# Selective scan: two of four summed terms move from TensorE to VectorE, and two sets of DMAs move in SyncE's queue

## The chip, the cores and the metric

One core of one Trainium2 chip runs the whole program. The metric is device microseconds of one execution. The profile comes from one further execution. Engines are called by the profile's names: PE is TensorE, DVE VectorE, ACT ScalarE, POOL GpSimd, SP SyncE, which here only issues DMAs.

## The reference

The program is four layers on x (4 batches of 512 tokens, 512 channels, fp32): a selective scan, a gated FFN with 4-bit weights, a cross attention, a ternary FFN, a mixing attention, a ternary FFN with norms, a second selective scan and a routed attention. The change touches only the two selective scans. For each batch they compute

```python
x = einsum('ed,bld->bel', in_proj_w, hidden)         # 512 channels x 512 steps
u = silu(depthwise_conv(x, 4 taps) + conv_b)
x_dbl = einsum('ke,bel->bkl', x_proj_w, u)           # rows: dt_low 16, B 16, C 16
delta = softplus(einsum('er,brl->bel', dt_proj_w, dt_low) + dt_proj_b)
state = state * exp(delta * A) + (delta * u) * B     # 512 steps, 16 states per channel
y = sum over states of state * C + D * u             # then times silu(z), added to x
```

softplus(v) is computed as max(v, 0) + log(1 + e), with e = exp(-|v|). Since 1 + e is rounded before the logarithm, the kernel adds the rounding error back: e + (1 - (1 + e)). So delta is a sum of four arrays: e, one-less = 1 - (1 + e), the logarithm, and the positive part.

## The kernel before, in words

`stage_mamba` runs twice, as "m0" (first scan stage, `then` set) and as "m3" (second, `given` set). Each goes through 4 batches b of NU = 32 units k. A unit is one state n of one half of the channels (2 blocks of 128 channels, 512 steps each), so n = 32 b + k counts units. In a unit ACT makes two decays `dA` (L757) into 3 PSUM banks, POOL makes the inputs `dB` = du * B (L777, 128x1024), DVE runs two scans (L827, L836) and one product with C (L844), POOL makes the other product (L766, 128x512), and PE adds both products to y in PSUM with an identity matmul (L570, L578). In units 5, 12, 21 and 28 DVE makes both products itself (L850). POOL writes `dB` up to four units ahead, but its queue holds dB(n), then product(n - 2), which waits for the scans of unit n - 2.

While batch b is scanned, the same engines prepare batch b + 1 at fixed units, given by tuples: projection, convolution, `xdbl`, step, and then delta. ACT makes |v| and the positive part, e (at units 21 and 22, into `xin`), one-more and one-less (22 to 24, into `du`), and the logarithm of both halves (24, into `delta`). PE then sums the four arrays for each of the 4 channel blocks ("sum", units `SUM`, two PSUM banks shared by everything that PE prepares), DVE multiplies a sum by u (`times_u`, L807, units `TIMES_U`) and ACT copies it out (`copy_sum`, L694, units `COPY_SUM`). A bank is free for the next item but one only when both have read it. The first stage prepares its batch 0 ahead of the loop, where nothing is being scanned, and prepares a fifth batch during its last one, which the second stage starts from; that one has 3 more to prepare. So 7 of the 8 batches have a preparation inside them. In m0's batch 2, PE and ACT also transpose and copy the next stage's weights (`REWEIGH`, L512 to L516, L621 to L625), among the same two banks.

SP loads B and C of a unit (`rows_of`, L427) into one of 5 buffers when the products of the unit five before are done. The rows come from DRAM: SP stores `xdbl` of a batch at the start of that batch (L445), waits until the store has landed, and goes on to the loads. In m0's batch 1 it first issues 8 loads of the next stage's weights.

Of the kernel before, what the change touches and what calls it, by code (L numbers as in the profile page):

```python
# [12 lines left out]
ALU = mybir.AluOpType  # L13
# [4 lines left out]
B, L, D = 4, 512, 512  # L18
# [277 lines left out]
def stage_mamba(chip, name, bc_dram, weights, then=None, given=None):  # L296
# [7 lines left out]
    EH = EB // 2  # L304
    FIRST, NB = 1 if given else 0, B + 1 if then else B
    NU = 2 * N
    with ExitStack() as st:
# [46 lines left out]
        s_dbl, s_dblc, s_bcd = sem("xdbl"), sem("xdbl_copied"), sem("bc_stored")  # L354
        s_relu = sem("relu")
        s_dt, s_ab, s_e, s_ln = sem("dt"), sem("dt_abs"), sem("dt_exp"), sem("dt_ln")
        s_one, s_back, s_sum, s_del, s_du = sem("one_more"), sem("one_less"), sem("summed"), sem("delta"), sem("du")
        s_bc = [sem(f"bc_loaded{i}") for i in range(NS)]
        s_dA, s_dB, s_sc = sem("dA"), sem("dB"), sem("scanned")
        s_hd, s_hp, s_ho = sem("product_dve"), sem("product_pool"), sem("product_own")  # L360
# [5 lines left out]
        GATED = (1, 3)  # L366
        PROJECT, TURN, CONV, XDBL, STEP = (0, 1, 2, 3), (5, 6, 11, 12), (7, 8, 9, 10), 13, (16, 17, 18, 19)
        SILU, EXP, ONE, BACK, LOG = (10, 13), (21, 22), (22, 23), (23, 24), 24
        SUM, TIMES_U, COPY_SUM = (24, 25, 27, 28), (26, 27, 29, 30), (28, 29, 31, 31)
        LAG = 3  # L370
        ROOT, INVERSE = 5, 7

        REWEIGH = {(0, 1): (0, 1), (0, 2): (2, 3)} if given else {(2, k): (i,) for i, k in enumerate((20, 21, 22, 25))} if then else {}
# [37 lines left out]
        @block.sync  # L411
        def _(sp):
            def park_or_load(i, h):
                part = parked[i][:, h * EH:(h + 1) * EH, :]
                here = (u, delta, du)[i][0][:, h * EH:(h + 1) * EH, :]
                if given:
                    sp.dma_start(here, part).then_inc(s_given[h] if i else s_gu, 16)
                else:
                    sp.dma_start(part, here).then_inc(s_park, 16)

            def rows_of(b, k):
                n, src = b * NU + k, bc_parked if b < FIRST else bc_dram[b]
                if n >= NS:
                    sp.wait_ge(s_hd, n - NS + 1)
                    sp.wait_ge(s_hp, n - NS + 1 - owned(n - NS + 1))
                    sp.wait_ge(s_ho, owned(n - NS + 1))
                sp.dma_start(BC[n % NS][:], src.rearrange("(w n) t -> n w t", w=2)[k % N:k % N + 1].broadcast_to(  # L427
                    [P, 2, L])).then_inc(s_bc[n % NS], 16)

            if given:  # L430
                weights.load_small(sp)
                for i in (2, 1):
                    park_or_load(i, 0)
                for k in range(2):
                    rows_of(0, k)
                park_or_load(0, 0)
                weights.load_rows(sp)
                for k in range(2, NS):
                    rows_of(0, k)
                for i in (2, 1, 0):  # L440
                    park_or_load(i, 1)
            for b in range(NB):
                if b >= FIRST:
                    sp.wait_ge(s_dblc, b + 1)
                    sp.dma_start(bc_parked if b == B else bc_dram[b], xdbl[R:W, :]).then_inc(s_bcd, 16)  # L445
                    sp.wait_ge(s_bcd, 16 * (b + 1 - FIRST))
                if b == B:
                    sp.wait_ge(s_du, NB * EB)
                    sp.wait_ge(s_del, NB * EB)
                    for i in range(3):  # L450
                        for h in range(2):
                            park_or_load(i, h)
                    sp.wait_ge(s_park, 96)
                    break
                if then and b == 1:
                    sp.wait_ge(s_wt, 1)
                    nxt.load_small(sp)
                    nxt.load_rows(sp)
                for k in range(NS if b < FIRST else 0, NU):
                    rows_of(b, k)  # L460

        def first_weights(pe):
            pe.wait_ge(weights.s_rows, weights.ROWS)
# [13 lines left out]
        def _(pe):  # L477
# [26 lines left out]
            def work(kind, b, i):  # L504
# [13 lines left out]
                elif kind == "project":  # L518
                    if i == 0 and b >= (FIRST if given else B):
                        pe.wait_ge(s_wgc, KC + 2)  # L520
                    for k in range(KC):
                        m = pe.matmul(out, in_T[:, k, i * P:(i + 1) * P],
                                      ctxT[:, k, b % B * L:(b % B + 1) * L], start=(k == 0), stop=(k == KC - 1))
                    m.then_inc(s_x, 1)
                elif kind == "conv":
                    pe.wait_ge(s_xin, b * EB + i + 1)
                    if given:
                        pe.wait_ge(s_pad, 2)
                        pe.wait_ge(s_diag, EB * TAPS)
                    elif b == B:  # L530
                        pe.wait_ge(s_diag, 2 * EB * TAPS)
                    for k in range(TAPS):
                        m = pe.matmul(out, taps[:, i, k, :], xin[:, i, k:k + L], start=(k == 0), stop=(k == TAPS - 1))
                    m.then_inc(s_conv, 1)
                elif kind == "xdbl":
                    pe.wait_ge(s_u, (b + 1) * EB)
                    for e in range(EB):
                        m = pe.matmul(out[0:W], x_T[:, e, :], u[b % 2][:, e, :], start=(e == 0), stop=(e == EB - 1))
                    m.then_inc(s_dbl, 1)
                elif kind == "step":  # L540
                    pe.wait_ge(s_dblc, b + 1)
                    pe.matmul(out, dt_T[:, i * P:(i + 1) * P], xdbl[0:R, :], start=True, stop=True).then_inc(s_dt, 1)
                elif kind == "sum":
                    pe.wait_ge(s_relu, b * EB + i + 1)
                    pe.wait_ge(s_back, 2 * b + i // EH + 1)
                    pe.wait_ge(s_ln, b + 1)
                    pe.matmul(out, ident[:], xin[:, i, TAPS - 1:], start=True, stop=False)
                    pe.matmul(out, ident[:], du[b % 2][:, i, :], start=False, stop=False)
                    pe.matmul(out, ident[:], delta[b % 2][:, i, :], start=False, stop=False)
                    pe.matmul(out, ident[:], positive[:, i, :], start=False, stop=True).then_inc(s_sum, 1)  # L550
                else:
                    for j in range(EH):
                        pe.wait_ge(s_yz[j], 2 * (b + 1))
                    for e in range(EB):
                        m = pe.transpose(out[:, e * P:(e + 1) * P], gate(b)[:, e, i * P:(i + 1) * P], ident[:])
                    m.then_inc(s_yt, 1)
# [228 lines left out]
        def _(dve):  # L785
# [11 lines left out]
                if not given:  # L797
                    diagonals(e, weights.small)
            if given:
                dve.sem_inc(s_du, EB)  # L800
            dve.wait_ge(s_pad, 2)
            norm.moments(dve)

            def times_u(b, e):
                dve.wait_ge(s_sum, b * EB + e + 1)
# [45 lines left out]

            if not given:
                norm.inverse(dve)
                for e in range(EB):
                    times_u(0, e)
            for b in range(B):
                for k in range(NU):
# [4 lines left out]
                    if b and k - 2 in TURN:  # L862
                        add_y(b - 1, TURN.index(k - 2))
                    if b + 1 < NB:
                        if k in TIMES_U:
                            times_u(b + 1, TIMES_U.index(k))
                    n = b * NU + k
# [2229 lines left out]
```

## Time and profile before

| | us |
|---|---|
| median of 3 runs | 4154.32 (4152.64 to 4157.45) |
| the profiled execution, its own time | 4150.07 |
| its span | 4148.3 |
| busy in the span: PE, DVE, ACT, POOL | 3649.8, 2860.9, 1818.7, 1435.3 |
| m0, starts of DVE's first and last unit | 96.08, 567.24 |
| m3, the same | 3160.05, 3607.62 |

A row of the timeline gives start, duration, engine, line, operation, output and inputs, and in brackets how long the engine had been idle before it and what ended the wait. Durations of neighbours on one engine overlap by about 0.1 us, so the pace of an engine is read from starts.

### The profile page before, as it was taken

What the parts mean: (1) busy time and instruction counts of PE and PEld (TensorE: products, weight loads), DVE (VectorE), ACT (ScalarE), POOL (GpSimd) and SP (SyncE); (2) the same over time, 40 slices, a digit from 0 to 9 for tenths busy, and PEclk for the clock granted to TensorE, in tenths of its full rate; (3) what the DMA queues carried; (4) which work ended last, traced back from release to release, by engine and by line L of the source; (5) the groups of instructions that cost most, each with busy time, mean ns of one, the idle gap of its engine ahead of it and who ended that gap; (6) DMA issues with size and microseconds to landing.
All of it is one profiled execution on the core that took longest, in us unless ns stands there. A gap on an engine that the chain in (4) does not pass through costs nothing. (4 is left out here: it accounts for less than half of the span.)

```text
span 4148.3 us, 47410 instructions
## 1 busy us (share of the span) xinstructions
PE 3649.8 (88%) x15419; PEld 1758.1 (42%) x15419; DVE 2860.9 (69%) x4137; ACT 1818.7 (44%) x3051; POOL 1435.3 (35%) x1030
## 2 busy tenths in 40 slices
PE   6999856999999999898999879785886999689898
PEld 2333323555555555542333344343333333244454
DVE  2888888578777884457888256627667899934663
ACT  4666542222222221243777443336665666321244
POOL 1999854122211220054000100003445999700122
PEclk8999987999999999997999989896998999899999
DMA  3555441122233212365775110001004555502420
GB/s 100 141 155 147 129 127 57 50 93 74 68 103 100 81 31 74 116 144 102 79 79 56 55 61 0 3 0 64 10 0 130 149 151 148 141 18 71 80 56 22
DMA packets 249833, 338.37 MB, mean 82 GB/s; under 512 B 45602, under 2 KB 147522, under 8 KB 248036
## 3 DMA queue, kind: packets, MB, share of 16 engines
q1 hardware_dynamic: 249620, 335.70, 32.5%
q8 instruction: 112, 1.84, 0.2%
q14 instruction: 101, 0.83, 0.1%
HBM read 284.38 MB, written 53.35 MB: 81 GB/s over the span
## 5 line engine op out<-in xcount | busy, mean ns | idle before, releaser
L757 ACT ACTIVATE m_dA<-m_delta,m_a_neg 128x512 f32<-128x512 f32 x512 | 347.2, 689 | 328.1 <-DVE m_H_bank L827 255.3
L1926 DVE TENSOR_REDUCE a_core_minus_max<-a_core_a 128x1 f32<-128x512 f32 x512 | 317.1, 684 | 57.2 <-PE a_core_a L1752 57.2
L570 PE MATMUL m_y<-m_H,ident 128*128 128x512 f32 x512 | 279.9, 634 | 80.9 <-DVE m_H L844 80.3
L777 POOL TENSOR_TENSOR m_dB<-m_du,m_BC 128x1024 f32<-128x1024 f32 x128 | 301.6, 2357 | 123.3 <-DVE m_du L807 84.7
L766 POOL TENSOR_TENSOR m_H<-m_H,m_BC 128x512 f32<-128x512 f32 x224 | 285.0, 1272 | 63.5 <-DVE m_H L836 60.6
L1878 ACT ACTIVATE X<-a_core_s 128x512 f32<-128x512 f32 x512 | 264.6, 603 | 92.7 <-PE a_core_s L1752 92.6
L777 POOL TENSOR_TENSOR XN<-m_du,m_BC 128x1024 f32<-128x1024 f32 x128 | 301.3, 2361 | 2.7 <-DMA m_BC<-bc_ready 2.7
L1318 POOL TENSOR_TENSOR ctxT<-ctxT,f_scales 128x1024 f32<-128x1024 f32 x48 | 103.7, 2159 | 531.7 <-DVE ctxT L1143 531.7
L578 PE MATMUL m_y<-m_H,ident 128*128 128x512 f32 x512 | 271.5, 619 | 2.5 <-POOL m_H L766 2.4
L1278 ACT ACTIVATE XN<-f_g,f_power_back 128x512 f32<-128x512 f32 x128 | 88.0, 687 | 404.1 <-PE f_g L1215 404.1
L1384 DVE SCALAR_TENSOR_TENSOR XN<-f_u,f_power_back,XN 128x512 f32<-128x512 f32 x128 | 95.8, 749 | 226.9 <-PE f_u L1215 226.9
L1289 ACT CAST f_inter_high<-XN 128x512 fp32r<-128x512 f32 x128 | 79.5, 621 | 383.5 <-DVE XN L1384 383.5
L1752 PE MATMUL a_core_a<-a_core_k,a_core_q 96*128 96x512 bf16 x512 | 209.2, 411 | 23.8 <-ACT a_core_max_rows L1896 10.1
L1205 PE MATMUL f_acc<-f_wdown_high,f_inter_high 128*128 128x512 f32 x512 | 224.1, 438 | 0.0
L1207 PE MATMUL f_acc<-f_wdown_high,f_inter_low 128*128 128x512 f32 x512 | 202.7, 396 | 0.0
L1326 POOL TENSOR_TENSOR XN<-f_mag,ctxT 128x1024 f32<-128x1024 f32 x48 | 127.7, 2660 | 215.8 <-DVE f_mag L1152 109.8
L1206 PE MATMUL f_acc<-f_wdown_low,f_inter_high 128*128 128x512 f32 x512 | 202.2, 395 | 0.0
L1213 PE MATMUL f_g<-f_xn_high,f_wh 128*128 128x512 f16 x512 | 196.5, 384 | 1.4 <-ACT f_wh L1191 1.4
L1752 PE MATMUL a_core_s<-a_core_q,a_core_k 98*128 98x512 bf16 x512 | 192.0, 386 | 4.8 <-ACT X L1878 4.5
L1213 PE MATMUL f_u<-f_xn_high,f_wh 128*128 128x512 f16 x512 | 194.6, 380 | 1.4 <-ACT f_wh L1191 1.4
L1214 PE MATMUL f_g<-f_xn_low,f_wh 128*128 128x512 f16 x512 | 195.1, 381 | 0.0
L1215 PE MATMUL f_g<-f_xn_high,f_wl 128*128 128x512 f16 x512 | 195.1, 381 | 0.0
(419 smaller groups left out, 8321.9 us busy)
## 6 DMA issues: line engine op xcount, KB each, us to landing
m_BC<-bc_rows SPq DMA_DIRECT2D x224, 512.0 KB, 4.9
XN<-in_L_ffn_w_dram SPq DMA_DIRECT2D x72, 256.0 KB, 2.7
m_BC<-bc_ready SPq DMA_DIRECT2D x32, 512.0 KB, 4.9
ternary<-ctxT SPq DMA_DIRECT2D x96, 128.0 KB, 1.7
a_core_q<-a_q_parts SPq DMA_DIRECT2D x48, 256.0 KB, 12.9
a_core_k<-a_k_parts SPq DMA_DIRECT2D x48, 256.0 KB, 14.6
f_w_tern<-ternary SPq DMA_DIRECT2D x24, 512.0 KB, 6.1
f_core_q<-f_q_parts SPq DMA_DIRECT2D x24, 512.0 KB, 8.1
```

Of the source, the lines that this page charges most:

```text
L570: pe.matmul(ps_y[:, 0, :], ident[:], HD[n % NH], start=False, stop=True, skip_group_check=True).then_inc(s_ad, 1)
L578: pe.matmul(ps_y[:, 1, :], ident[:], HP[n % NH], start=False, stop=True, skip_group_check=True).then_inc(s_ap, 1)
L757: act.activation(dA[:, i % NA, :], delta[b % 2][:, e, :], ACT.Exp, scale=a_neg[:, e, k % N:k % N + 1]).then_inc(s_dA, 1)
L766: pool.tensor_tensor(HP[n % NH], HP[n % NH], BC[n % NS][:, 1, :], ALU.mult).then_inc(s_hp, 1)
L777: pool.tensor_tensor(dB[n % ND][:], du[b % 2][:, h * EH:(h + 1) * EH, :], BC[n % NS][:, 0:1, :].broadcast_to([P, EH, L]), ALU.mult).then_i ...
L1205: pe.matmul(ps_acc[:, t, :], high, DH[gb][:, q % 4, :], start=(q % 4 == 0), stop=False)
L1206: pe.matmul(ps_acc[:, t, :], high, DL[gb][:, q % 4, :], start=False, stop=False)
L1207: m = pe.matmul(ps_acc[:, t, :], low, DH[gb][:, q % 4, :], start=False, stop=(q % 4 == 3))
L1213: pe.matmul(out, w[0], xh[:, k, toks], start=(k == 0), stop=False)
L1752: pe_last = pe.matmul(out[:, cols], lhs(c, k), rhs(c, k), start=(c == 0), stop=(c == NCH - 1 and mask is None))
L1878: act.activation(prob[pair][e][:, j, q0:], ps_s[:, at % NR, q0:], ACT.Exp, scale=hs.scale).then_inc(s_exp, 1)
L1926: dve.tensor_reduce(mx[u % 2][:, qt, h:h + 1], ps_a[:, at % NR, 0:n], AX.X, ALU.max, negate=True).then_inc(s_red, 1)
```

## The change

`error` is new: for each half of the channels (128x1024) DVE adds e to one-less in place, waits for its own result, and adds the positive part in place. Both operands of both adds lie in SBUF. It runs for the next batch ahead of the scans of units 24 and 25. PE's sum has two matmuls left. `SUM`, `TIMES_U` and the first `COPY_SUM` units move one unit later. SP stores `xdbl` of batch b + 1 ahead of the load for unit 22 of batch b and waits for it only at the batch's start; the 8 loads of the next stage's weights come behind unit 8's load of batch 1.

```diff
-        SUM, TIMES_U, COPY_SUM = (24, 25, 27, 28), (26, 27, 29, 30), (28, 29, 31, 31)
-        LAG = 3
+        ERROR, SUM, TIMES_U, COPY_SUM = (24, 25), (25, 26, 27, 28), (27, 28, 29, 30), (29, 30, 31, 31)
+        LAG, STORE = 3, 22
...
-            for b in range(NB):
+            def store_rows(b):
+                sp.wait_ge(s_dblc, b + 1)
+                sp.dma_start(bc_parked if b == B else bc_dram[b], xdbl[R:W, :]).then_inc(s_bcd, 16)
+
+            if not given:
+                store_rows(0)
+            for b in range(B):
                 if b >= FIRST:
-                    sp.wait_ge(s_dblc, b + 1)
-                    sp.dma_start(bc_parked if b == B else bc_dram[b], xdbl[R:W, :]).then_inc(s_bcd, 16)
                     sp.wait_ge(s_bcd, 16 * (b + 1 - FIRST))
...
                 for k in range(NS if b < FIRST else 0, NU):
+                    if k == STORE and b + 1 < NB:
+                        store_rows(b + 1)
                     rows_of(b, k)
+                    if then and (b, k) == (1, NU // 4):
+                        sp.wait_ge(s_wt, 1)
+                        nxt.load_small(sp)
+                        nxt.load_rows(sp)
...
-                    pe.wait_ge(s_back, 2 * b + i // EH + 1)
+                    pe.wait_ge(s_err, 2 * b + i // EH + 1)
                     pe.wait_ge(s_ln, b + 1)
-                    pe.matmul(out, ident[:], xin[:, i, TAPS - 1:], start=True, stop=False)
-                    pe.matmul(out, ident[:], du[b % 2][:, i, :], start=False, stop=False)
-                    pe.matmul(out, ident[:], delta[b % 2][:, i, :], start=False, stop=False)
-                    pe.matmul(out, ident[:], positive[:, i, :], start=False, stop=True).then_inc(s_sum, 1)
+                    pe.matmul(out, ident[:], du[b % 2][:, i, :], start=True, stop=False)
+                    pe.matmul(out, ident[:], delta[b % 2][:, i, :], start=False, stop=True).then_inc(s_sum, 1)
...
+            def error(b, h):
+                rows = slice(h * EH, (h + 1) * EH)
+                t = du[b % 2][:, rows, :]
+                dve.wait_ge(s_back, 2 * b + h + 1)
+                dve.tensor_tensor(t, t, xin[:, rows, TAPS - 1:], ALU.add).then_inc(s_eh, 1)
+                dve.wait_ge(s_relu, b * EB + (h + 1) * EH)
+                dve.wait_ge(s_eh, 2 * b + h + 1)
+                dve.tensor_tensor(t, t, positive[:, rows, :], ALU.add).then_inc(s_err, 1)
...
+                for h in range(2):
+                    error(0, h)
                 for e in range(EB):
                     times_u(0, e)
...
+                        if k in ERROR:
+                            error(b + 1, ERROR.index(k))
                         if k in TIMES_U:
                             times_u(b + 1, TIMES_U.index(k))
```

On DVE, in m0's batch 0, units 23 to 27 stand so before (two scans and a product are a unit; the unit of BC3 is 23, that of BC4 is 24):

```order
L844 TENSOR_TENSOR m0_H<-m0_H_bank,m0_BC3 128x512
L827 SCALAR_TENSOR_TENSOR m0_H_bank<-m0_dA,m0_dB0 128x512
L836 SCALAR_TENSOR_TENSOR m0_H<-m0_dA,m0_dB0 128x512
L844 TENSOR_TENSOR m0_H<-m0_H_bank,m0_BC4 128x512
L827 SCALAR_TENSOR_TENSOR m0_H_bank<-m0_dA,m0_dB1 128x512
L836 SCALAR_TENSOR_TENSOR m0_H<-m0_dA,m0_dB1 128x512
L844 TENSOR_TENSOR m0_H<-m0_H_bank,m0_BC0 128x512
L807 TENSOR_TENSOR m0_du1<-m0_w,m0_u1 128x512
```

The same place on DVE with the change, where XN as an input of an add is the positive part:

```order
L860 TENSOR_TENSOR m0_H<-m0_H_bank,m0_BC3 128x512
L815 TENSOR_TENSOR m0_du1<-m0_du1,m0_xin 128x1024
L818 TENSOR_TENSOR m0_du1<-m0_du1,XN 128x1024
L843 SCALAR_TENSOR_TENSOR m0_H_bank<-m0_dA,m0_dB0 128x512
L852 SCALAR_TENSOR_TENSOR m0_H<-m0_dA,m0_dB0 128x512
L860 TENSOR_TENSOR m0_H<-m0_H_bank,m0_BC4 128x512
L815 TENSOR_TENSOR m0_du1<-m0_du1,m0_xin 128x1024
L818 TENSOR_TENSOR m0_du1<-m0_du1,XN 128x1024
L843 SCALAR_TENSOR_TENSOR m0_H_bank<-m0_dA,m0_dB1 128x512
L852 SCALAR_TENSOR_TENSOR m0_H<-m0_dA,m0_dB1 128x512
L860 TENSOR_TENSOR m0_H<-m0_H_bank,m0_BC0 128x512
```

Two adds of 128x1024 stand ahead of unit 24's scans and two ahead of unit 25's, and the first times_u no longer follows unit 25 but unit 26.

On PE, in m0's batch 2, around the last reweigh item (L516, the weights `dt_rows`), the order before is:

```order
L547 MATMUL m0_w<-m0_xin,ident 128x512
L548 MATMUL m0_w<-m0_du1,ident 128x512
L549 MATMUL m0_w<-m0_delta1,ident 128x512
L550 MATMUL m0_w<-XN,ident 128x512
L578 MATMUL m0_y<-m0_H,ident 128x512
L570 MATMUL m0_y<-m0_H,ident 128x512
L516 MATMUL m0_w<-ident,m0_dt_rows 16x128 x4
L547 MATMUL m0_w<-m0_xin,ident 128x512
L548 MATMUL m0_w<-m0_du1,ident 128x512
L549 MATMUL m0_w<-m0_delta1,ident 128x512
L550 MATMUL m0_w<-XN,ident 128x512
```

And with the change:

```order
L524 MATMUL m0_w<-ident,m0_dt_rows 16x128 x4
L555 MATMUL m0_w<-m0_du1,ident 128x512
L556 MATMUL m0_w<-m0_delta1,ident 128x512
L584 MATMUL m0_y<-m0_H,ident 128x512
L576 MATMUL m0_y<-m0_H,ident 128x512
L555 MATMUL m0_w<-m0_du1,ident 128x512
L556 MATMUL m0_w<-m0_delta1,ident 128x512
```

The first sum stood ahead of the reweigh item and now stands behind it, so the second sum's bank is no longer the one that the first sum used, but the one that the reweigh item used.

## Rows read from the trace of the kernel before

**Rows 1.** The page: the span

```profile
span 4148.3 us, 47410 instructions
```

**Rows 2.** Tile m_H_bank: what ended DVE's idle time (us, times)

```profile
  ACT m_dA L757: 71.1, 98
...
  POOL m_dB L777: 5.2, 13
```

**Rows 3.** Timeline, DVE, m0's batch 1: last product of unit 23, units 24, 25

```profile
297.48 0.67 DVE L844 TENSOR_TENSOR m_H<-m_H_bank,m_BC 128x512 f32<-128x512 f32 x1
...
300.67 1.23 DVE L827 TENSOR_TENSOR_SCAN m_H_bank<-m_dA,m_dB 128x512 f32<-128x512 f32 x1 [2.52 <-ACT m_dA L757]
...
303.79 1.23 DVE L827 TENSOR_TENSOR_SCAN m_H_bank<-m_dA,m_dB 128x512 f32<-128x512 f32 x1 [0.20 <-ACT m_dA L757]
```

**Rows 4.** Timeline, POOL, the same stretch

```profile
296.35 2.35 POOL L777 TENSOR_TENSOR m_dB<-m_du,m_BC 128x1024 f32<-128x1024 f32 x1
298.67 1.26 POOL L766 TENSOR_TENSOR m_H<-m_H,m_BC 128x512 f32<-128x512 f32 x1
299.89 2.35 POOL L777 TENSOR_TENSOR XN<-m_du,m_BC 128x1024 f32<-128x1024 f32 x1
303.09 1.27 POOL L766 TENSOR_TENSOR m_H<-m_H,m_BC 128x512 f32<-128x512 f32 x1 [0.85 <-DVE m_H L836]
```

**Rows 5.** Timeline, the 4-bit FFN: POOL beside DVE with all operands in SBUF

```profile
687.35 2.95 POOL L1326 TENSOR_TENSOR XN<-f_mag,ctxT 128x1024 f32<-128x1024 f32 x1 [4.10 <-issue]
...
687.96 2.89 DVE L1139 TENSOR_SCALAR ctxT<-f_packed 128x1024 int32<-128x1024 int32 x1
...
692.18 1.93 POOL L1318 TENSOR_TENSOR ctxT<-ctxT,f_scales 128x1024 f32<-128x1024 f32 x1 [1.89 <-DVE ctxT L1143]
...
692.19 2.47 DVE L1374 TENSOR_TENSOR f_inter_low<-XN,f_inter_high 128x512 fp32r<-128x512 f32 x1
...
696.56 1.23 DVE L1152 SCALAR_TENSOR_TENSOR f_mag<-ctxT,f_mag 128x1024 f32<-128x1024 int32 x1
```

**Rows 6.** Timeline, the last ternary FFN: two POOL products in a row, DVE's copy

```profile
2922.57 3.41 POOL L2877 TENSOR_TENSOR f_h_gained<-XN 128x512 f32<-128x512 f32 x2 [2.08 <-DVE XN L2904]
...
2924.85 1.15 DVE L2894 COPY f_gate_up_scale<-f_gate_up_scale 128x2 f32<-128x2 f32 x1
...
2925.93 1.27 POOL L2877 TENSOR_TENSOR f_h_gained<-XN 128x512 f32<-128x512 f32 x1
```

**Rows 7.** Timeline, SP, POOL and DVE at m0's border from batch 0 to 1

```profile
195.79 0.46 SPq L445 DMA_DIRECT2D bc_rows<-m_xdbl  x1
...
204.46 17.82 SPq L427 DMA_DIRECT2D m_BC<-bc_rows  x6
...
211.21 2.35 POOL L777 TENSOR_TENSOR m_dB<-m_du,m_BC 128x1024 f32<-128x1024 f32 x1 [5.36 <-issue]
...
213.59 1.23 DVE L827 TENSOR_TENSOR_SCAN m_H_bank<-m_dA,m_dB 128x512 f32<-128x512 f32 x1 [1.97 <-POOL m_dB L777]
...
220.67 1.23 DVE L827 TENSOR_TENSOR_SCAN m_H_bank<-m_dA,XN 128x512 f32<-128x512 f32 x1 [0.62 <-POOL XN L777]
```

**Rows 8.** Timeline, DVE and ACT in m0's batch 2, units 24 to 30

```profile
420.82 1.23 DVE L827 TENSOR_TENSOR_SCAN m_H_bank<-m_dA,m_dB 128x512 f32<-128x512 f32 x1 [4.39 <-ACT m_dA L757]
...
429.74 0.56 ACT L694 COPY m_delta<-m_w 128x512 f32<-128x512 f32 x1
...
436.30 0.69 DVE L807 TENSOR_TENSOR m_du<-m_w,m_u 128x512 f32<-128x512 f32 x1 [6.01 <-PE m_w L550]
...
448.31 0.69 DVE L807 TENSOR_TENSOR m_du<-m_w,m_u 128x512 f32<-128x512 f32 x1 [0.85 <-PE m_w L550]
```

**Rows 9.** Timeline, DVE and PE ahead of m0's loop: sums and times_u

```profile
76.80 2.04 PE L547 MATMUL m_w<-m_xin,ident 128*128 128x512 f32 x2 [11.77 <-ACT m_delta L689]
...
78.60 0.17 DVE L257 SCALAR_TENSOR_TENSOR m_norm_shift<-m_norm_mv,m_norm_rstd 128x16 f32<-128x16 f32 x1
...
92.31 0.69 DVE L807 TENSOR_TENSOR m_du<-m_w,m_u 128x512 f32<-128x512 f32 x1 [2.74 <-PE m_w L550]
```

More of the change, by code:

```diff
@@ L356, in stage_mamba @@
         s_dt, s_ab, s_e, s_ln = sem("dt"), sem("dt_abs"), sem("dt_exp"), sem("dt_ln")
-        s_one, s_back, s_sum, s_del, s_du = sem("one_more"), sem("one_less"), sem("summed"), sem("delta"), sem("du")
+        s_one, s_back, s_err, s_sum, s_del, s_du = (sem(n) for n in (
+            "one_more", "one_less", "error", "summed", "delta", "du"))
+        s_eh = sem("error_half")
         s_bc = [sem(f"bc_loaded{i}") for i in range(NS)]
@@ L441, in _ @@
                     park_or_load(i, 1)
-            for b in range(NB):
+            def store_rows(b):
[4 more added lines that the diff above has]
+            for b in range(B):
                 if b >= FIRST:
-                    sp.wait_ge(s_dblc, b + 1)
-                    sp.dma_start(bc_parked if b == B else bc_dram[b], xdbl[R:W, :]).then_inc(s_bcd, 16)
                     sp.wait_ge(s_bcd, 16 * (b + 1 - FIRST))
[L447 to L458, printed above, removed]
                 for k in range(NS if b < FIRST else 0, NU):
+                    if k == STORE and b + 1 < NB:
+                        store_rows(b + 1)
                     rows_of(b, k)
+                    if then and (b, k) == (1, NU // 4):
+                        sp.wait_ge(s_wt, 1)
+                        nxt.load_small(sp)
+                        nxt.load_rows(sp)
+            if then:
+                sp.wait_ge(s_du, NB * EB)
+                sp.wait_ge(s_del, NB * EB)
+                for i in range(3):
+                    for h in range(2):
+                        park_or_load(i, h)
+                sp.wait_ge(s_park, 96)
+                sp.wait_ge(s_bcd, 16 * NB)
         def first_weights(pe):
@@ L799, in _ @@
             if given:
-                dve.sem_inc(s_du, EB)
+                for sem_, count in ((s_eh, 2), (s_err, 2), (s_du, EB)):
+                    dve.sem_inc(sem_, count)
             dve.wait_ge(s_pad, 2)
             norm.moments(dve)
+            def error(b, h):
[6 more added lines that the diff above has]
+                dve.tensor_tensor(t, t, positive[:, rows, :], ALU.add).then_inc(s_err, 1)
             def times_u(b, e):
@@ L853, in _ @@
                 norm.inverse(dve)
+                for h in range(2):
+                    error(0, h)
                 for e in range(EB):
```

## The prediction

> **What bounds the kernel now.** The change touches the two scan stages alone, some 960 us of the span [rows 1], so I read these. First the tile view of the PSUM bank that DVE's scans write, because every unit passes through DVE's two scans and product: of its idle time there, ACT's decays ended 71.1 us and POOL's dB 5.2 us [rows 2]. Then the timelines of DVE and POOL side by side at units 23 to 25, where the adds go. With nothing in the way a DVE unit repeats every 3.12 us (300.67 to 303.79) [rows 3]. POOL's pair, dB and product, repeats every 3.54 us (296.35 to 299.89), but it skips the product in 4 of 32 units and waits 0.85 us for a scan here [rows 4]. So DVE sets the pace, in part through ACT: ahead of unit 24 it stands 2.52 us, because ACT makes the logarithm before unit 24's decays [rows 3]. POOL is almost without a gap. It is not the bound, but nearly so, and it is nearly always inside an instruction. That matters for what follows.
>
> **Price of an add.** DVE has no 128x1024 add with both inputs in SBUF before. The nearest row with the same shape and two SBUF inputs took 1.23 us [rows 5]. The question is what it costs beside POOL. There DVE's L1374 (128x512, two SBUF inputs) was issued 0.01 us behind a POOL product and took 2.47 us; POOL's ended at 694.11, DVE's at 694.66 [rows 5]. So DVE stood until POOL was through, then ran its 0.55 us. The other way round, POOL's product at 687.35 took 2.95 us, 0.60 more than the 2.35 of its kind in [rows 4], while DVE's L1139, issued at 687.96 right behind another DVE instruction, took 2.89 us and ended 0.55 us after POOL's [rows 5]. So a waiting POOL gets in between two DVE instructions. And a waiting DVE gets in between two of POOL: the copy of 2 elements issued at 2924.85 ended at 2926.00, with POOL's second product, and not after its third, which started at 2925.93 [rows 6]. The scans and products of the loop have one operand in PSUM, and POOL runs beside them unhindered [rows 3, 4]. The adds have none there. I take strict turns: an add waits for POOL's running instruction, runs about 1.1 us from its end, and POOL's next waits that long.
>
> The Trainium skill has two statements on this. "SBUF — State Buffer", section "Who interferes with whom", says that a DVE instruction with two SBUF inputs and a GpSimd one that reads SBUF exclude each other for a whole instruction; by it the sum is the one below. "Advanced Engine Details and Errata", section "VectorE Performance Modes", names only two-port modes as interfering, in which an fp32 add of two tensors does not run; by it the change would cost what the first rival gives. The trace agrees with the first: L1374 took 2.47 us.
>
> **Unit 24's pair**, at m0's batch 1. DVE issues the first add when the product of unit 23 is nearly through (298.07). POOL's dB ends at 298.70. The add runs to about 299.8; POOL's product, which would have started at 298.67, to 301.0; the second add, which must wait for the first, to 302.15. The scan then starts at 302.1 in place of 300.67: the 2.52 us stall for ACT hides most of it, +1.4.
>
> **Unit 25's pair** has no cover. POOL's dB, which started at 299.89, now runs from 302.15 to 304.5, its product of unit 24 (which needs that unit's second scan, through at 304.4) to 305.7. DVE's unit ends at 304.9; the first add waits to 305.7 and runs to 306.8; POOL's next dB takes the port until 309.2; the second add ends at 310.3. The scan of unit 25 starts there in place of 303.79: +6.5 in all, +5.1 from this pair. Afterwards POOL waits for unit 25's scan, so it is not late itself; it has lost 4 x 1.1 us of 113 and the gap of 0.85, while DVE lost 6.5, so DVE stays the bound. Behind DVE, ACT's three PSUM banks, PE's y adds and SP's loads of B and C all follow at the new pace.
>
> Six batches are of this kind (m0's 0, 1, 3; m3's 0, 1, 2): 6 x 6.5 = +39. Where within POOL's instruction the first add falls moves this by about 1 us a batch.
>
> **m0's batch 2.** ACT is busier, DVE's wait ahead of unit 24 is 4.39 us (scan at 420.82) and hides the first pair but for 0.9 us; the second costs 5.0. But the 6.01 us that DVE waits ahead of unit 27 for the second sum [rows 8] should go. That sum needed the bank of the first, which ACT's copy freed at 430.3 (429.74 + 0.56), and PE then needed four matmuls. Now its bank comes free with ACT's copy of the reweigh item at the head of its unit 28, which hangs on unit 26's first scan alone; the sum then needs two matmuls, and DVE asks for it only after unit 27, some 4 us later. The later 0.85 us wait goes too. 0.9 + 5.0 - 6.0 - 0.85 = -1.
>
> **Ahead of the loop.** Sums went every 3.43 us (0.69 and a wait of 2.74), four matmuls each [rows 9], so a matmul is 0.86 us warm and a sum will be 1.72. The adds can't start before DVE has computed the norm's shift (78.77); POOL is idle, so the four take 1.2 us each, to 83.6. The first sum starts with the first half, at 81.3 in place of 76.80, with TensorE slow after its idle time as in the row of 76.80 (a pair of passes in 2.04 us in place of 1.02 us), and ends near 84.6; the second at 86.3, the third 88.0, the fourth 89.8. The last times_u starts at 89.8 in place of 92.31: -2.5.
>
> **SP.** At m0's border to batch 1 the store was issued at 195.79, the first load of B and C only at 204.46, and POOL stood 5.36 us until 211.21. DVE then waited 1.97 us and, POOL being late, 0.62 us three times, of which one is shown [rows 7]; against the 0.2 that it waits anyway these are 1.8 + 3 x 0.4 plus a little at the gated products, -3.3. No other border shows such a wait, so there the earlier store gives nothing. The 8 weight loads, behind unit 8's load in batch 1, delay the next loads of B and C by a microsecond or two; POOL needs them later than that, so I take 0.5 and 0 to 2 as bounds.
>
> PE loses 64 matmuls (8 x 4 x 2), 55 us of work, at nothing gained elsewhere: in ordinary batches no wait of DVE for a sum stands in the trace.
>
> **Sum.** -2.5 + 39 - 1 - 3.3 + 0.5 = +32.7. The profiled execution took 4150.07 us, so 4182.8; the median stands 4.25 us above that execution, so 4187.
>
> **Rivals.**
> 1. The adds run beside POOL without waiting. Against it stand the rows of L1374 and L1139 [rows 5]; for it, only that neither is this very instruction. Then unit 24's pair (2.4 us) vanishes in the stall of 2.52, unit 25's costs 2.3: 6 x 2.3 = 13.8; batch 2 gives 2.3 - 6.9 = -4.6; with the rest -2.5 + 13.8 - 4.6 - 3.3 = +3.4, 4158: not slower by what can be measured. It decides if an add shows under 1.3 us while POOL runs.
> 2. POOL is not made to yield between two instructions, and an add waits until POOL has to wait for something. In batch 1 POOL would run to 302.3, both adds follow to 304.5 (+3.8), and at unit 25 POOL runs product and dB to 310.4, the adds to 312.6: +8.8 a batch, 52.8 in six, sum +46.5, 4201. Against it stands the copy of 2924.85 [rows 6], but it is a tiny one.
> 3. Turns as forecast, but batch 2's stall stays, since the new bank is freed by ACT too: +6.9, 4194.
> 4. PE's freed time shortens the loop. The trace shows DVE waiting for PE in no ordinary batch's sums, so this would need waits that I don't see. On rival 1's prices, and with unit 25's pair hidden too (2.3 us in each of seven batches), it would be 3.4 - 16.1 = -12.7, 4142.
>
> **How the numbers follow.** The forecast 0.62, rival 2 0.13, rival 3 0.09, rival 1 0.09, rival 4 0.04, others 0.03. What a measurement of this kernel can tell from no change is about 0.2%, 8.3 us. Slower: the forecast and rivals 2 and 3 with a little, 0.86; same: rival 1, 0.10; faster 0.04. The forecast's own range is 4178 to 4196 (1 us a batch either way, and the opening). For 8 in 10 I take 4172 to 4202, which holds rivals 2 and 3 and cheap pairs (4 us a batch: 24 - 6.3 = +18), and leaves out rivals 1 and 4.
>
> **What would show it.** The adds' own durations: 1.2 us ahead of the loop, 1.8 to 3.6 in it. POOL's instructions beside them lengthened by about 1.1 us, four a batch. First scan of unit 24 late by 1 to 2 us with its wait for ACT gone, that of unit 25 late by 6 to 7. No wait of 6 us for a sum in m0's batch 2. No POOL gap of 5 us at the border to batch 1. Sums at 1.72 us. Adds of 1.2 us in the loop, or a scan of unit 25 late by under 3 us, would make the prediction wrong.

## The result and the profile after

The changed kernel took 4197.6 us in the median of 4 runs (4196.34 to 4204.6), the kernel before 4155.89 in 4 runs taken with it: a ratio of 1.011 (95% interval 1.0098 to 1.0123), slower by 41 to 51 us (41.7 between the medians). In what follows, ratios leave out two executions that stood far off, and medians hold them: 9393.38 us in experiment 1, and 4235.75 us of the kernel before in experiments 3 to 6. The page of the profiled execution (4204.6 us), beside [rows 1], and the answer for the tile of the scans' PSUM bank, beside [rows 2]:

```profile
span 4202.9 us, 47205 instructions
PE 3623.3 (86%) x15291; PEld 1742.2 (41%) x15291; DVE 2943.4 (70%) x4169; ACT 1818.7 (43%) x3051; POOL 1445.1 (34%) x1030
```

```profile
  ACT m_dA L763: 52.3, 94
...
  POOL m_dB L783: 1.6, 6
```

DVE waits less than before (52.3 us for ACT in place of 71.1, 1.6 for POOL in place of 5.2), and the kernel is slower: the time is inside DVE's own instructions. The groups by line and shape, DVE, show where (busy us, mean ns of one | idle before):

```profile
L815 DVE TENSOR_TENSOR m_du<-m_du,m_xin 128x1024 f32<-128x1024 f32 x16 | 49.6, 3100 | 0.0
L818 DVE TENSOR_TENSOR m_du<-m_du,XN 128x1024 f32<-128x1024 f32 x16 | 35.3, 2203 | 1.7
L823 DVE TENSOR_TENSOR m_du<-m_w,m_u 128x512 f32<-128x512 f32 x32 | 21.9, 684 | 5.5 <-PE m_w L556 5.5
```

The means of 3.1 and 2.2 us hide four lengths, of about 1.2, 1.9, 3.2 and 5.2 us. The timeline of DVE at m0's batch 1, from the last product of unit 23 to the scan of unit 25, answers to [rows 3]:

```profile
303.43 0.67 DVE L860 TENSOR_TENSOR m_H<-m_H_bank,m_BC 128x512 f32<-128x512 f32 x1
304.01 5.25 DVE L815 TENSOR_TENSOR m_du<-m_du,m_xin 128x1024 f32<-128x1024 f32 x1
309.37 1.23 DVE L818 TENSOR_TENSOR m_du<-m_du,XN 128x1024 f32<-128x1024 f32 x1
310.51 1.23 DVE L843 TENSOR_TENSOR_SCAN m_H_bank<-m_dA,m_dB 128x512 f32<-128x512 f32 x1
...
313.34 1.93 DVE L815 TENSOR_TENSOR m_du<-m_du,m_xin 128x1024 f32<-128x1024 f32 x1
315.37 3.18 DVE L818 TENSOR_TENSOR m_du<-m_du,XN 128x1024 f32<-128x1024 f32 x1
318.48 1.22 DVE L843 TENSOR_TENSOR_SCAN m_H_bank<-m_dA,m_dB 128x512 f32<-128x512 f32 x1
```

And POOL beside it, which answers to [rows 4]:

```profile
302.29 2.37 POOL L783 TENSOR_TENSOR m_dB<-m_du,m_BC 128x1024 f32<-128x1024 f32 x1
304.61 1.28 POOL L772 TENSOR_TENSOR m_H<-m_H,m_BC 128x512 f32<-128x512 f32 x1
305.82 2.36 POOL L783 TENSOR_TENSOR XN<-m_du,m_BC 128x1024 f32<-128x1024 f32 x1
312.92 1.27 POOL L772 TENSOR_TENSOR m_H<-m_H,m_BC 128x512 f32<-128x512 f32 x1 [4.74 <-DVE m_H L852]
314.14 3.33 POOL L783 TENSOR_TENSOR XN<-m_du,m_BC 128x1024 f32<-128x1024 f32 x1
320.89 1.27 POOL L772 TENSOR_TENSOR m_H<-m_H,m_BC 128x512 f32<-128x512 f32 x1 [3.41 <-DVE m_H L852]
```

Read them together. The first add was issued at 304.01, inside a dB that ended at 304.66. It didn't run then: product and second dB follow with their plain 1.28 and 2.36 us, POOL's chain ends at 308.18 because the next product needs a scan that stands behind the add, and the add ends 1.08 us later, at 309.26. The second add finds POOL idle: 1.23 us. The second pair goes otherwise: its first add, issued at 313.34 inside a product that ended at 314.19, runs 1.1 us from there, and POOL's dB is the one that waits (3.33 us in place of 2.35).

Against before, by the starts of the first scans, this batch lost 3.90 us at unit 24 and 4.85 at unit 25. The six ordinary batches lost 8.65, 8.74 and 8.73 (m0's 0, 1, 3) and 9.33, 8.72 and 8.17 (m3's), 52.3 in all. Some of the spread in m3 isn't the change's (the landing of the first B and C, and 0.5 us that before itself lost at the end of its batch 2). In m0's batch 2, DVE's timeline at units 24 to 28, which answers to [rows 8], has no wait for a sum. The last two lines are the first and the second times_u:

```profile
430.65 1.92 DVE L815 TENSOR_TENSOR m_du<-m_du,m_xin 128x1024 f32<-128x1024 f32 x1
432.68 3.18 DVE L818 TENSOR_TENSOR m_du<-m_du,XN 128x1024 f32<-128x1024 f32 x1
435.78 1.22 DVE L843 TENSOR_TENSOR_SCAN m_H_bank<-m_dA,m_dB 128x512 f32<-128x512 f32 x1
...
449.70 0.68 DVE L823 TENSOR_TENSOR m_du<-m_w,m_u 128x512 f32<-128x512 f32 x1
...
453.20 0.69 DVE L823 TENSOR_TENSOR m_du<-m_w,m_u 128x512 f32<-128x512 f32 x1
```

At the border to batch 1, the timelines of SP, POOL and DVE answer to [rows 7]: the store goes out at 160.56, POOL waits 1.51 us for a scan in place of 5.36, DVE's first scan waits 0.20 in place of 1.97.

```profile
160.56 0.46 SPq L446 DMA_DIRECT2D bc_rows<-m_xdbl  x1
...
213.14 1.27 POOL L772 TENSOR_TENSOR m_H<-m_H,m_BC 128x512 f32<-128x512 f32 x1 [1.51 <-DVE m_H L852]
...
220.39 1.23 DVE L843 TENSOR_TENSOR_SCAN m_H_bank<-m_dA,m_dB 128x512 f32<-128x512 f32 x1 [0.20 <-ACT m_dA L763]
```

Ahead of the loop, beside [rows 9], the four adds take 1.22 and 1.23 us, and the times_u go at 85.20, 87.73, 89.45 and 91.17:

```profile
81.42 2.04 PE L555 MATMUL m_w<-m_du,ident 128*128 128x512 f32 x2 [16.46 <-DVE m_du L818]
83.25 1.92 PE L556 MATMUL m_w<-m_delta,ident 128*128 128x512 f32 x2
84.96 1.88 PE L555 MATMUL m_w<-m_du,ident 128*128 128x512 f32 x2
86.67 1.03 PE L556 MATMUL m_w<-m_delta,ident 128*128 128x512 f32 x2
```

The profiled executions differ by 54.6 us of span, more than the medians, since the one of the changed kernel lies 7.0 us above its median and the one before 5.8 us below: -1.1 to m0's first scan, +22.8 in m0, +5.4 between the two stages, +27.5 in m3. The +5.4 arises in stages whose code is the same. In the experiments below it is +1.2 to +7.9 where DVE makes the adds (or experiment 3's operations in their place) and -0.3 to +0.7 where it doesn't; what carries it there isn't shown.

### The profile page after: what moved, and what is told of

Same layout as the page of the kernel before. It is cut to its first block and busy times, and to the rows that moved or that the text cites. A ratio compares the mean times of both kernels' runs of the same rounds, so it can differ in the third digit from the quotient of the medians.

```text
span 4202.9 us, 47205 instructions
## 1 busy us (share of the span) xinstructions
PE 3623.3 (86%) x15291; PEld 1742.2 (41%) x15291; DVE 2943.4 (70%) x4169; ACT 1818.7 (43%) x3051; POOL 1445.1 (34%) x1030
## 5 line engine op out<-in xcount | busy, mean ns | idle before, releaser
L576 PE MATMUL m_y<-m_H,ident 128*128 128x512 f32 x512 | 289.5, 653 | 155.8 <-DVE m_H L860 155.2
L584 PE MATMUL m_y<-m_H,ident 128*128 128x512 f32 x512 | 271.9, 620 | 0.0
L576 PEld LDWEIGHTS m_y<-m_H,ident 128*128 128x128 f32 x512 | 93.8, 200 | 319.4 <-DVE m_H L860 254.7
L1234 PE MATMUL f_u<-f_xn_low,f_wh 128*128 128x512 f16 x512 | 195.1, 381 | 0.0
```

What stands on the lines that cost most here:

```text
L576: pe.matmul(ps_y[:, 0, :], ident[:], HD[n % NH], start=False, stop=True, skip_group_check=True).then_inc(s_ad, 1)
L584: pe.matmul(ps_y[:, 1, :], ident[:], HP[n % NH], start=False, stop=True, skip_group_check=True).then_inc(s_ap, 1)
```

## The experiments

Theory after the result: an add with both operands in SBUF and a POOL instruction exclude each other, and who goes next isn't by turns. Rivals: strict turns, with something else behind the 5.25 us; no exclusion, but a cost of the adds' place in the order.

**1. The store and the loads alone** (before, with only SP's part of the change):

```diff
...
                 for k in range(NS if b < FIRST else 0, NU):
+                    if k == STORE and b + 1 < NB:
+                        store_rows(b + 1)
                     rows_of(b, k)
+                    if then and (b, k) == (1, NU // 4):
...
```

> The kernel before with SP's part of the change alone (early store of B and C's rows, weight loads behind unit 8 of batch 1). If the border to batch 1 of the first stage is all that it touches, POOL's gap of 5.4 us there goes and the time falls by 2.9 us (what the changed kernel's scan starts gained there), to about 4153 where before is 4156. Rival: the moved weight loads delay B and C in batch 1 and give it back: no difference, and a gap of POOL near unit 9 that DVE waits for.

Measured: 4150.28 in 11 runs beside 4150.03 in 21, ratio 0.9999 (0.9989 to 1.0008). In its trace the border to batch 1 gives 2.85 us back (first scan of unit 4 in batch 1), as in the changed kernel (2.84). Of that, up to 1.7 us goes and comes again with a wait of DVE for ACT at unit 10 of a batch, which is 2.6 or 4.3 us long in kernels with and without the change. So the trace shows the gain, and the times, with an interval of some 4 us either way, can't tell it from nothing.

**2. POOL held back.** The changed kernel, with two waits on POOL:

```diff
+                    if b + 1 < NB and k - 3 == ERROR[0]:
+                        pool.wait_ge(s_err, 2 * (b + 1) + 2)
                     pool.wait_ge(s_bc[n % NS], 16 * (n // NS + 1))
...
+                    if b + 1 < NB and k - 1 == ERROR[0]:
+                        pool.wait_ge(s_err, 2 * (b + 1) + 1)
                     if n >= 2:
                         product(n - 2)
```

> The changed kernel with two waits added on POOL: its product of unit 23 waits for the first pair of adds, its dB of unit 27 for the second. Theory dry queue: the first add took 5.2 us because POOL went through all that it had ready (rest of dB, product, dB) before DVE got in, although POOL stood idle for 4.7 us right behind. With POOL held back the first pair takes 1.7 and 1.2 us and costs under 0.5 us a batch in place of 3.9, the second 1.9 and 1.2 us and 3.0 in place of 4.9: 3.5 us a batch in place of 8.7, 4169. Rival strict turns with some other delay of the first add: it keeps about 5 us, and the time does not fall, or rises since POOL is late.

Measured: 4174.69 in 4 runs, ratio 1.0056 (1.0041 to 1.0071), half of the loss gone: an ordinary batch of m0 lost 4.1 to 4.2 us, where 3.5 was expected. DVE and POOL at m0's batch 1 (the adds are L819 and L822 here), two pieces of each:

```profile
298.40 1.76 DVE L819 TENSOR_TENSOR m_du<-m_du,m_xin 128x1024 f32<-128x1024 f32 x1
300.27 1.22 DVE L822 TENSOR_TENSOR m_du<-m_du,XN 128x1024 f32<-128x1024 f32 x1
...
304.24 1.98 DVE L819 TENSOR_TENSOR m_du<-m_du,m_xin 128x1024 f32<-128x1024 f32 x1
306.32 2.10 DVE L822 TENSOR_TENSOR m_du<-m_du,XN 128x1024 f32<-128x1024 f32 x1
```

```profile
302.79 2.34 POOL L785 TENSOR_TENSOR XN<-m_du,m_BC 128x1024 f32<-128x1024 f32 x1
305.10 2.24 POOL L772 TENSOR_TENSOR m_H<-m_H,m_BC 128x512 f32<-128x512 f32 x1
```

With POOL's next instruction held, the first add starts as soon as the running dB is through: its 5.25 us came from POOL's two next instructions. But the second pair's first add, issued inside a dB with a product right behind it, did get in between the two. So "POOL never yields while it has work" is wrong as well. What differs: here POOL had paused 2.49 us right ahead of the instruction before this dB. Ahead of the first pair's add it had run 18 instructions without a pause, and was in the nineteenth. That add got in, since POOL stood held behind it. The second pair's second add took 2.10 us and not the expected 1.2, since it waited for the product: the rest of the missed 3.5.

**3. One operand from PSUM.** In the loop both adds become operations of the same size that read du from SBUF and the scans' bank, times zero, from PSUM. The first multiplies du by that zero, the second adds it; so the sum leaves out e, one-less and the positive part, and the output is another one. One wait of DVE for its own result is added at the pair's end.

```diff
-                dve.tensor_tensor(t, t, xin[:, rows, TAPS - 1:], ALU.add).then_inc(s_eh, 1)
...
+                    dve.scalar_tensor_tensor(out=t, in0=bank_, scalar=0.0, in1=t, op0=ALU.mult, op1=ALU.mult).then_inc(s_eh, 1)
...
-                dve.tensor_tensor(t, t, positive[:, rows, :], ALU.add).then_inc(s_err, 1)
...
+                    dve.scalar_tensor_tensor(out=t, in0=bank_, scalar=0.0, in1=t, op0=ALU.mult, op1=ALU.add).then_inc(s_err, 1)
+                    dve.wait_ge(s_err, 2 * b + h + 1)
```

> Edit: in the loop the two adds become operations of the same 128x1024 size that read one operand from SBUF (du) and the other from PSUM (the bank of the scans, times zero), so the sum that PE forms is the logarithm without its error and the positive part (the output is not the reference's). The same waits, and one more at the pair's end, stay. Theory (two operands in SBUF are what makes an add wait for a POOL instruction): both operations take 1.2 to 1.4 us wherever they stand, POOL's neighbours keep 2.35 and 1.25 us, an ordinary batch loses about 2.3 us (the first pair is hidden by the stall for ACT), ratio near 1.002. Rival (the adds wait for POOL's queue whatever their operands are, or it is their place in the order that costs): 5.2, 1.2, 1.9 and 3.2 us as in the changed kernel, ratio near 1.011.

Measured: 4160.12 in 10 runs beside 4152.35 in 13, ratio 1.0018 (1.0009 to 1.0028). All 28 operations in the loop took 1.21 to 1.23 us; at m0's batch 1, in the midst of the same chain of POOL (its dB is the first line):

```profile
294.12 2.37 POOL L783 TENSOR_TENSOR m_dB<-m_du,m_BC 128x1024 f32<-128x1024 f32 x1
...
295.67 1.21 DVE L819 SCALAR_TENSOR_TENSOR m_du<-m_H_bank,m_du 128x1024 f32<-128x1024 f32 x1
296.98 1.23 DVE L825 SCALAR_TENSOR_TENSOR m_du<-m_H_bank,m_du 128x1024 f32<-128x1024 f32 x1
298.38 1.23 DVE L851 TENSOR_TENSOR_SCAN m_H_bank<-m_dA,m_dB 128x512 f32<-128x512 f32 x1 [0.17 <-DVE m_du L825]
```

POOL's dB beside them kept 2.36 us. The first pair cost 0.1 us, the second 2.3. So it isn't the place. But the kind of operation changed with the operand, from TENSOR_TENSOR to SCALAR_TENSOR_TENSOR, which is a rival. The trace of the kernel before has the same kind with both operands in SBUF, in the 4-bit FFN:

```profile
611.37 2.31 POOL L1318 TENSOR_TENSOR ctxT<-ctxT,f_scales 128x1024 f32<-128x1024 f32 x1 [40.45 <-DVE ctxT L1143]
```

```profile
611.92 2.83 DVE L1148 SCALAR_TENSOR_TENSOR f_mag<-ctxT,f_mag 128x1024 f32<-128x1024 int32 x1
```

It ended at 614.75, 1.07 us behind POOL's product; the same line took 1.21 to 1.23 us the 42 times that POOL was idle at its issue. And the TENSOR_TENSOR products of the loop (L844), with one operand in PSUM, took 0.66 to 0.69 us beside a busy or an idle POOL. So the kind falls too, and the two SBUF operands are the cause.

**4. All four adds ahead of unit 24.**

```diff
-                        if k in ERROR:
-                            error(b + 1, ERROR.index(k))
+                        if k == ERROR[0]:
+                            for h in range(2):
+                                error(b + 1, h)
```

> Edit: all four adds of a batch stand ahead of unit 24's second part, none ahead of unit 25. Theory (a DVE instruction that finds POOL in a chain without pauses waits until POOL's queue has to stop; the ones behind it then run beside an idle POOL): the first add takes about 5.2 us, the other three 1.2 us each; the scan of unit 24 is late by some 6.3 us, that of unit 25 by no more, so an ordinary batch loses 6.2 us in place of 8.7, ratio near 1.007. Rival (strict turns, DVE gets in after each POOL instruction): first add 1.7, second 2.3, third 3.4, fourth 1.2 us, and POOL instructions between them.

Measured: 4187.32 in 4 runs, ratio 1.0086 (1.0067 to 1.0106). DVE at m0's batch 1:

```profile
299.12 5.56 DVE L815 TENSOR_TENSOR m_du<-m_du,m_xin 128x1024 f32<-128x1024 f32 x1
304.78 1.23 DVE L818 TENSOR_TENSOR m_du<-m_du,XN 128x1024 f32<-128x1024 f32 x1
305.93 1.22 DVE L815 TENSOR_TENSOR m_du<-m_du,m_xin 128x1024 f32<-128x1024 f32 x1
307.25 1.23 DVE L818 TENSOR_TENSOR m_du<-m_du,XN 128x1024 f32<-128x1024 f32 x1
```

One long wait, then three adds beside an idle POOL, 6.3 to 7.0 us a batch in place of 8.7 (6.2 was expected). Strict turns are out.

**5. The first pair one unit earlier.**

```diff
-        ERROR, SUM, TIMES_U, COPY_SUM = (24, 25), (25, 26, 27, 28), (27, 28, 29, 30), (29, 30, 31, 31)
+        ERROR, SUM, TIMES_U, COPY_SUM = (23, 25), (25, 26, 27, 28), (27, 28, 29, 30), (29, 30, 31, 31)
```

> Edit: the first pair of adds stands ahead of unit 23 in place of 24; the second pair stays. There the first add is issued about 0.2 us before a dB of POOL ends, with the product and the next dB ready behind it. Strict turns: the add takes about 1.3 us. Turn at the end of the product: about 2.5 us. Theory (no turn until POOL's chain stops): 4.8 us or more.

One execution, 4202.94 us. The first add took 4.82 to 5.02 us in five of the six ordinary batches, though the dB that ran at its issue had only 0.2 to 0.4 us to go; in m3's batch 0, where POOL had just paused 0.20 us, it took 1.93.

**6. One short pause in POOL's chain.** The changed kernel with one wait more, for a scan that ends at about that time:

```diff
+                    if b + 1 < NB and k == 25:
+                        pool.wait_ge(s_sc, 2 * (n - 2) + 1)
                     pool.wait_ge(s_bc[n % NS], 16 * (n // NS + 1))
```

> Edit: POOL gets one wait more, ahead of the dB at its unit 25, for the first scan of DVE's unit 23, which is through at about that moment: a pause of some 0.2 us in POOL's chain, two instructions ahead of the first add. Theory (a waiting DVE gets in between two POOL instructions only when POOL has paused for a semaphore within the last few instructions): the first add takes about 1.9 us, the second 2.2, and the scan of unit 24 is late by 1.4 to 1.6 us as forecast at first. Rival (the add waits until POOL's queue has nothing ready, however recently it paused): the first add still takes about 5 us, and the scan of unit 24 is late by 3.9 us.

One execution, 4180.68 us. POOL and DVE at m0's batch 1 (adds L817, L820):

```profile
297.58 2.36 POOL L785 TENSOR_TENSOR m_dB<-m_du,m_BC 128x1024 f32<-128x1024 f32 x1 [0.17 <-DVE m_H_bank L845]
...
299.89 2.25 POOL L772 TENSOR_TENSOR m_H<-m_H,m_BC 128x512 f32<-128x512 f32 x1
302.11 3.32 POOL L785 TENSOR_TENSOR XN<-m_du,m_BC 128x1024 f32<-128x1024 f32 x1
```

```profile
299.05 1.97 DVE L817 TENSOR_TENSOR m_du<-m_du,m_xin 128x1024 f32<-128x1024 f32 x1
301.13 2.10 DVE L820 TENSOR_TENSOR m_du<-m_du,XN 128x1024 f32<-128x1024 f32 x1
303.15 1.22 DVE L845 TENSOR_TENSOR_SCAN m_H_bank<-m_dA,m_dB 128x512 f32<-128x512 f32 x1
```

The same instructions in the same order, with the product and the next dB as ready as before, and 0.17 us of pause ahead (0.17 to 2.46 us in the seven batches): the first add takes 1.96 to 1.98 us in all seven, the second 2.10. The scan of unit 24 is 1.49 us late, that of unit 25 another 4.83, and every ordinary batch of m0 loses 6.3 us, the forecast's 6.5 but for 0.2.

**7. How far back may the pause be?** As experiment 6, with the pause at another unit in each batch, twice, with the places exchanged:

```diff
+            PAUSE = {(0, 19), (1, 18), (2, 24)} if given else {(0, 22), (3, 20), (1, 21)}
...
+                    if (b, k) in PAUSE:
+                        pool.wait_ge(s_sc, 2 * (n - 2) + (1 if k == 24 else 2))
```

> Edit: as in the run with POOL's pause, but the one extra wait of POOL stands at another unit in each ordinary batch, so that the pause lies a different number of POOL instructions ahead of the first add. First stage: unit 22 in batch 0 (the add is issued in the sixth instruction behind the pause), unit 21 in batch 1 (eighth), unit 20 in batch 3 (tenth). Last stage: unit 19 in batch 0 (twelfth), unit 18 in batch 1 (fourteenth), unit 24 in batch 2 (third). Theory (how lately POOL has paused decides): short adds of about 1.9 us up to some distance, long ones of about 5.2 us beyond it, with one border; the third gives 1.9, the fourteenth 5.2, and between them the run tells. Rival (only a pause right ahead of the instruction in which the add is issued matters): all but perhaps the third take 5.2 us.

> Edit: as the run before it, with the places exchanged between batches and stages. First stage: unit 18 in batch 0, unit 20 in batch 1, unit 24 in batch 3. Last stage: unit 22 in batch 0, unit 21 in batch 1, unit 19 in batch 2. Theory (the distance decides, not the batch): each distance gives the same length of the first add as in the run before it. Rival (it is something of the batch, such as its loads): the batches keep their lengths and the distances do not.

One execution each, 4195.49 and 4200.5 us. From the timelines of DVE and POOL, the length of the first add by the position, counted from the pause, of the POOL instruction in which it was issued (1 is experiment 6, 19 the changed kernel):

| position behind the pause | first add, us | less the rest of the running instruction |
|---|---|---|
| 1 | 1.96 to 1.98 | 1.1 |
| 3 | 2.39, 2.39 | 1.1 |
| 6 | 2.09, 2.08 | 1.1 |
| 8 | 2.51, 2.53 | 1.1 |
| 10 | 2.63, 6.16 | 1.1, 4.6 |
| 12 | 6.55, 6.56 | 4.6 |
| 14 | 6.68, 6.68 | 4.6 |
| 19 (31 in experiment 4's batch shown) | 5.19 to 5.54 (5.56) | 4.6 |

The batch doesn't matter, the distance does. The border lies at 10 instructions (17.3 us), where the same distance gave both; each other distance of these two runs stands on two adds. The two first adds at it, first run, then second:

```profile
546.04 2.63 DVE L819 TENSOR_TENSOR m_du<-m_du,m_xin 128x1024 f32<-128x1024 f32 x1
```

```profile
306.35 6.16 DVE L819 TENSOR_TENSOR m_du<-m_du,m_xin 128x1024 f32<-128x1024 f32 x1
```

The pauses ahead of them were 0.85 and 0.84 us. The rival of the first run (only a pause right ahead counts) and that of the second (it is the batch) both fall.

**8. The stall of 6 us in m0's batch 2 by itself.** Experiment 1 with the last reweigh item two units earlier:

```diff
-        REWEIGH = {(0, 1): (0, 1), (0, 2): (2, 3)} if given else {(2, k): (i,) for i, k in enumerate((20, 21, 22, 25))} if then else {}
+        REWEIGH = {(0, 1): (0, 1), (0, 2): (2, 3)} if given else {(2, k): (i,) for i, k in enumerate((20, 21, 22, 23))} if then else {}
```

> The kernel before with SP's part of the change, and the last reweigh item of the first stage's batch 2 at unit 23 in place of 25; sums stay at four matmuls on PE and no add goes to DVE. If the 6.0 us wait for the second sum came only from which bank that sum has, it goes (DVE's wait for sums in batch 2 under 1 us), and the time is 6 to 7 us under the run with SP's part alone, 4146 where before is 4156. Rival: PE's four matmuls were the reason, then a wait of 3 us or more stays and the time falls by 3 us or less.

> Edit: none against the run that moved the last reweigh item to unit 23 on top of the earlier store; it is timed once more on another occasion. If that run's gain is real, the ratio to the kernel before is 0.998 to 0.9995 again; if it was chance, 0.9995 to 1.0005.

Measured: 4145.04 in 11 runs, ratio 0.9989 (0.998 to 0.9998), and again 4145.92 in 11 beside 4151.31 in 15, ratio 0.9988 (0.9979 to 0.9997): some 5 us faster than the kernel before both times, and the best of all that ran. DVE's wait for the second sum, 6.01 us in [rows 8], is 1.63 us here, and one of 1.32 us is new ahead of the first:

```profile
426.12 0.69 DVE L813 TENSOR_TENSOR m_du<-m_w,m_u 128x512 f32<-128x512 f32 x1 [1.32 <-PE m_w L556]
...
431.27 0.69 DVE L813 TENSOR_TENSOR m_du<-m_w,m_u 128x512 f32<-128x512 f32 x1 [1.63 <-PE m_w L556]
```

That is 3.0 us net in m0's batch 2, with the border's 2.85 from the store beside it. Under 1 us of waiting was expected, and 6 to 7 us less than experiment 1; it came to 2.95 us of waiting and, with 4145.04 against 4150.28, 5.2 us less. The wait for the bank is gone: the second sum's matmuls stand right behind PE's own for y, where before they stood behind ACT's copy and 5.00 us of idle time:

```profile
430.36 2.08 PE L547 MATMUL m_w<-m_xin,ident 128*128 128x512 f32 x2 [5.00 <-ACT m_delta L694]
```

But the bank isn't the whole of it. Counted from unit 24's scan, the sum starts only 0.7 us earlier than before. The other 2.3 of the 3.0 us are its four matmuls, 3.6 us at a granted clock of 1.00 (2.4 GHz) here, 5.9 before, where the clock was 0.50 (1.2 GHz) up to 434.0. The slow stretch went to the first sum: that one stands behind 4.03 us of idle time here, runs at 0.50, and is the new wait. What the bank costs without the clock isn't shown.

## Why the prediction was right, and where it was not

Slower was right, and the size in part: +32.7 us was forecast, +41.7 measured between the medians, 4187 against 4197.6. The forecast's own range, 4178 to 4196, misses it by 1.6; the wide one, to 4202, holds it because it was drawn to hold the second rival too, and half of that rival came true. By its steps:

- **The adds exclude POOL** (against the first rival, 4158). Right. Experiment 3 is the proof: same size, same place, one operand from PSUM, 1.21 to 1.23 us. The Trainium skill, "SBUF — State Buffer", section "Who interferes with whom", calls this an exclusive lock on the pair of ports that DVE and GpSimd share; the runs agree that the two exclude each other, and can't show the ports. The Trainium skill, "Advanced Engine Details and Errata", section "VectorE Performance Modes", names two-port modes alone; the add of 5.25 us, an fp32 one of two tensors, shows that they are not the only ones.
- **Strict turns.** This is the step that failed, in the first pair only. "A waiting DVE gets in between two of POOL" was taken from [rows 6], and there POOL had waited 2.08 us just before; in [rows 5] it had waited 4.10 and 1.89 us. Every row that the prediction had for a turn stood right behind a pause. Ahead of unit 24 POOL has run 18 instructions without one, and there the add waits until POOL's chain stops: 5.25 us and +3.90 for the pair, against +1.4 forecast. The second rival gave exactly this for the first pair (+3.8), but for the wrong reason in general: at the second pair, behind a pause, turns hold.
- **Unit 25's pair.** Forecast +5.1, measured +4.85. Right, and in its way: the first add waited 0.85 us for a product (0.8 forecast), the second for a whole dB. Only what stood ahead of that product was otherwise, an idle POOL (4.74 us) in place of a dB. In experiment 6, where the first pair went by turns too, the second cost 4.83.
- **Six batches.** Forecast 39, measured 52.3. The difference, 13, is six times 2.5 from the first pair, 15, less 1.5 by which the second pair was cheaper. With the pause of experiment 6 the batch costs 6.3, so the arithmetic was right and its rule was not.
- **m0's batch 2.** Forecast -1, measured -1.75 from unit 23 to the next batch: the first pair +0.7 (0.9 forecast), the second +4.85 (5.0), the wait for the second sum -6.1 (-6.0), the later one and the rest -1.2 (-0.85). Here POOL had waited 1.20 us just before the adds, so turns held. DVE's idle time for sums fell from 18.8 us over the kernel to the 5.5 of the group shown. The third rival, that the stall stays, is out, by a narrow margin: the second sum's two matmuls started 3.8 us before DVE asked, as forecast, but took 3.8 us and not 1.7, at a granted clock of 0.50 (1.2 GHz) behind 1.54 us of idle time.
- **Border.** -3.3 forecast, -2.84 measured, and -2.85 by itself in experiment 1.
- **Weight loads.** +0.5 forecast, nothing measured: POOL shows a gap of 2.83 us at 247.88 in batch 1, and DVE's unit starts don't move by it.
- **Ahead of the loop.** -2.5 forecast; the first scan came 1.1 us earlier. The forecast had one pair of passes at the slow clock. It lasted over the first sum and half of the second: pairs took 2.04, 1.92 and 1.88 us, with a granted clock of 0.50 and 0.51 (1.2 GHz) from 81.4 to 86.7, before one took 1.03 at 1.00. The other traces with this opening start their first scan at 94.81 to 96.78, and those with the old one at 96.08 (before), 98.34 (experiment 1), 96.51 and 96.10 (experiment 8), so this term can't be told from the spread.
- **PE's freed time** gave nothing that shows, as forecast: outside the opening and batch 2 the kernel before has one wait for a sum, of 0.43 us, so the fourth rival has nothing to live on.

With the measured prices, -1.1 + 52.3 - 1.75 - 2.85 = +46.6; the ratio's centre is 0.011 x 4155.89 = +45.7, the medians differ by 41.7, and the profiled executions by 54.6, of which 8.0 has no term here: the 5.4 between the stages, and 2.6 inside them.

What stays open is why ten instructions are the border. The runs tell distance from batch, from the pause's length (0.17 to 4.7 us) and from what is ready behind it, but not whether the chip counts instructions or time, since POOL's chain is the same in all. Nor do they tell "until POOL stops" from "two instructions more": behind every long add POOL's chain stopped after just two, and where experiment 2 stopped it at once the add went at once.

## What to carry to other kernels

Before an elementwise operation is moved to DVE, look whether both its inputs lie in SBUF and POOL is busy beside it: then its price isn't its own 1.2 us but 2 to 6.7, and POOL's next instruction may pay as well; with one input in PSUM it cost 1.2. Take the price from a row where the neighbour is in the same condition, with no pause for as long, and not merely of the same kind. And where an engine's stall hangs on a shared bank, move the other user of the bank first: one number in a table gave 5 us, with the earlier store, where the whole change, 64 matmuls fewer for 32 adds more, cost some 46 by the ratio.

## What the runs showed of the hardware

POOL doesn't give way to a waiting DVE in the same manner at all times. Within 8 instructions of a pause of its own, DVE got in right behind the running instruction every time, and POOL's next took 1.0 us longer. From the twelfth on, POOL's next two ran undisturbed, and the add, 1.1 us of work, took 4.8 to 6.7 us; there POOL had to wait. At the tenth both were seen. A pause of 0.17 us right ahead of the running instruction was enough for the turn. By that, waits added to POOL made the kernel faster: a ratio to the kernel before of 1.0056 (1.0041 to 1.0071) in experiment 2 against 1.011 (1.0098 to 1.0123), and 4180.68 us in the one execution of experiment 6 against 4197.6.
